# Ten score groups a batch instead of twelve, x cast at another place, the first stack DMA in three pieces, and another opening order of FFN 0

## The reference

```
x = x + 0.5 * ffn(layernorm(x))                 # "FFN 0" in the code (phase 0)
x = x + attention_block(layernorm(x))           # block = its input + gate * attention
x = x + 0.5 * ffn(layernorm(x))                 # "FFN 1" (phase 1)

ffn(y)       = (silu(y Wg^T) * (y Wu^T)) Wd^T   # 128 -> 384 -> 128, int weights / 127
attention(y) : h = rmsnorm(y) * norm_w; 4 query heads, 2 key/value heads of 32
               q, k normalised to length 1; scores = q k^T * exp(log_temperature)
               causal mask; softmax; times v; times Wo; times gate
```

## Time and profile before

| | us |
|---|---|
| median of 3 runs (lowest, highest) | 457.25 (456.99, 458.0) |
| the profiled execution | 457.19 |
| its span, first to last instruction | 455.4 |
| PE busy | 413.0 (91%) |
| ACT busy | 381.8 (84%) |
| DVE busy | 354.6 (78%) |
| POOL busy | 260.2 (57%) |
| first score of batch 0 | at 102.5 |
| first gate product of FFN 1 | at 372.95 |

### The profile page before, as it was taken

How to read it: one execution, slowest core, us unless ns; L and a number is a source line. 1 busy time by engine, 2 the same in 40 slices (tenths; PEclk the granted TensorE clock), 3 DMA queues, 4 the chain that set the end, 5 groups by cost and what they waited for, 6 DMA issues and landing times.

```text
span 455.4 us, 10469 instructions
## 1 busy us (share of the span) xinstructions
PE 413.0 (91%) x3747; PEld 213.8 (47%) x3747; DVE 354.6 (78%) x873; ACT 381.8 (84%) x545; POOL 260.2 (57%) x321
## 2 busy tenths in 40 slices
PE   0679998989998999999999999999999999999995
PEld 0346665764334335335335335335334344666654
DVE  5899997799499779689689689688556938878654
ACT  3799999667968988988988988988987999999960
POOL 5499999973544444444444444441140466998951
PEclk9999999999999999999999999999999999999999
DMA  5596433434028072074072072082070034557462
GB/s 161 127 165 150 71 48 69 71 71 97 20 51 136 1 138 51 1 129 59 0 138 46 0 138 47 1 134 54 1 140 0 2 48 57 129 95 139 93 116 74
DMA packets 119150, 34.94 MB, mean 77 GB/s; under 512 B 101568, under 2 KB 119104, under 8 KB 119104
## 3 DMA queue, kind: packets, MB, share of 16 engines
q1 hardware_dynamic: 117824, 34.02, 39.9%
q10 hardware_dynamic: 1280, 0.33, 0.3%
HBM read 4.98 MB, written 4.19 MB: 20 GB/s over the span
## 4 chain that ended last, share of the span: by engine, by line
PE 52%; issue 13%; ACT 13%; DVE 11%; POOL 7%; DMA 2%; DVEq 0%; SPq 0%; POOLq 0%; ACTq 0%
PE ps L508 11%; PE ps L709 11%; PE ps L690 9%; PE ps L714 9%; ACT XN L458 4%; PE ps L572 3%; PE ps L561 3%; ACT PT L820 3%; PE ps L597 3%; DVE H L327 2%; ACT SG L476 2%; DVE X L1024 2%; PE ps L694 2%; POOL OL L281 2%; DVE AN L1011 1%
## 5 line engine op out<-in xcount | busy, mean ns | idle before, releaser
L820 ACT ACTIVATE PT<-ps,k_exp 128x1024 f32<-128x1024 f32 (+1 forms) x192 | 162.0, 899 | 20.2 <-PE ps L694 14.8
L508 PE MATMUL ps<-XT,WT 128*128 128x512 f16 x384 | 94.4, 384 | 6.8 <-DVE H L327 2.4
L690 PE MATMUL ps<-QKT 128*128 128x512 f16 (+3 forms) x384 | 87.1, 328 | 11.4 <-ACT PT L820 9.3
L709 PE MATMUL ps<-PT,V 128*32 128x512 f32 (+3 forms) x768 | 81.8, 498 | 0.0
L714 PE MATMUL ps<-PT,ones 128*32 128x512 f32 (+3 forms) x768 | 79.6, 486 | 0.0
L433 POOL TENSOR_TENSOR HL<-H,HH 128x1024 f16<-128x1024 f32 x31 | 66.5, 2146 | 6.4 <-ACT HH L482 3.6
L327 DVE SCALAR_TENSOR_TENSOR H<-SG,k_isilu,ps 128x1536 f32<-128x1536 f32 x32 | 58.0, 1812 | 13.6 <-ACT SG L476 5.9
L281 POOL TENSOR_TENSOR OL<-ON,OH 128x512 f16<-128x512 f32 x15 | 18.2, 1215 | 77.4 <-ACT OH L277 77.4
L690 PEld LDWEIGHTS ps<-QKT 128*128 128x128 f16 x384 | 27.8, 97 | 69.3 <-ACT PT L820 60.2
L508 PEld LDWEIGHTS ps<-XT,WT 128*128 128x128 f16 x384 | 34.4, 98 | 51.8 <-issue 8.8
L458 ACT ACTIVATE XN<-X,NB,RS 128x128 f32<-128x128 f32 x128 | 52.4, 483 | 2.7 <-POOL NB L405 2.7
(11 more groups left out here) (139 smaller groups left out, 645.6 us busy)
## 6 DMA issues: line engine op xcount, KB each, us to landing
result<-X SPq DMA_DIRECT2D x15, 256.0 KB, 2.5
X<-in_L_attn_x SPq DMA_DIRECT2D x7, 512.0 KB, 4.8
X<-in_L_attn_x SPq DMA_DIRECT2D x2, 256.0 KB, 5.1
XT<-w_int SPq DMA_TRANSPOSE x32, 3.1
AXT<-AS SPq DMA_TRANSPOSE x16, 2.8
QKT<-ST SPq DMA_TRANSPOSE x16, 5.6
w_int<-in_L_ffn_w_gate SPq DMA_DIRECT2D x1, 192.0 KB, 4.2
w_int<-in_L_ffn_w_up SPq DMA_DIRECT2D x1, 192.0 KB, 4.5
```

The costliest lines, as they stand in the source:

```text
L508: i = e.matmul(out[:, j, :], WT[:, wp, w * NJ + j, :], XT[k % 2][:, xp, :], start=a == 0, stop=a == len(passes) - 1)
L690: i_ = e.matmul(o, QKT[k % 2][:, i // TPC, NH + hp, i % TPC * P:(i % TPC + 1) * P], QKT[k % 2][:, qc, 2 * hp + h, CH - n:CH], start=True, ...
L709: e.matmul(PVD[HD * h:HD * h + HD, 0, CH - n:CH], V[k % 2][:, i, v0:v0 + HD], PT[g % 2][:, h, 0:n], start=i == 0, stop=done, skip_group_ch ...
L820: e.activation(PT[g % 2][:, 2 * hp:2 * hp + 2, 0:n], SCORES[hp][:, :, 0:n], ACT.Exp, scale=k_exp[:, 0:1]).then_inc(a_exp, 1)
```

## The change

1. **Groups.** A group is now a list of tiles, each with its key tile, its offset in the score and PT buffers, and its width. In each `qc` the 384-wide and the 128-wide tile share one group (512 columns); the 256-wide tile comes last. `NG` is 10, `G0` is 3. `USES`, `MOVED` and the group numbers in ACT's program are renumbered: `("wo", 1)` in group 2, `("wo", 0)` in group 9 (the last; it was the last but one).
2. **ACT in attention.** `o_hi` of the batch before in group 1 (was 2). The squares of the second half in group 2, behind its exponentials (they were in group 1 behind the V copies). `stack_hi` in groups 4 and 5. Both `x_hi` in group 8. In batch 0 the QKV work starts in group 2 (was 3), `stack_hi` stands in groups 6 and 7, `x_hi(2)` and `x_hi(3)` in groups 0 and 1; `x_hi(2)` was ahead of the first exponentials.
3. **First stack DMA.** The DMA that turns ST[0] of batch 0 is issued as three, of two heads each: keys, first two query heads, last two. The first half of the first scores waits for the first two, the second half for the third.
4. **FFN 0's opening.** POOL makes the factors of chunks 2 to 5 one chunk at a time (was: 2 and 3 together). ACT does normalise(2) and x_hi(2) ahead of silu(0), and silu(1) ahead of h_hi(0). DVE copies the low parts r = 3, 4 behind the stats of chunk 4. Some steps of the attention's first rows and weights move by one step.

```diff
         def group(g):
             ph, c = divmod(g, NC)
-            return [0, 1, 2, 2, 3, 4][c] if g < 6 else 2 + c // 2 if not ph else NC // 2 + 2 + c // 2
+            return c if g < 6 else 3 + c // 2 if not ph else NC // 2 + 3 + c // 2
...
             def rstd_pair(k, c):
-                if not ph and c in (4, 5):
+                if not ph and 2 <= c < 6:
                     rstd(k, c, 1)
...
-            early = [(normalise, 0), (normalise, 1), (x_hi, 0), (x_hi, 1), (silu, 0)]
-            if ph:
-                early += [(normalise, 2), (x_hi, 2), (silu, 1)]
+            early = [(op, c) for c in range(3) for op in (normalise, x_hi)] + [(silu, 0), (silu, 1)]
...
-        groups = [(qc, i) for qc in range(QCS) for i in range(TPC * (qc + 1))]
+        def row_groups(qc):
+            d = TPC * qc
+            return [[(i, 0, CH)] for i in range(d + 1)] + \
+                [[(d + 1, 0, 3 * P), (d + 3, 3 * P, P)], [(d + 2, 0, 2 * P)]]
+
+        groups = [(qc, tiles_) for qc in range(QCS) for tiles_ in row_groups(qc)]
...
         USES = {0: [("qkv", 0, 0), ("qkv", 0, 1)], 1: [("qkv", 1, 0), ("qkv", 1, 1)],
-                3: [("wo", 1)], 8: [("rows", 0)], 10: [("wo", 0)], 11: [("rows", 1)]}
+                2: [("wo", 1)], 7: [("rows", 0)], 9: [("wo", 0), ("rows", 1)]}
-        MOVED = {0: [], 1: [], 3: USES[0], 4: USES[1]}
+        MOVED = {0: [], 1: [], 2: USES[0], 3: USES[1]}
...
+                if g == 0 and isinstance(b, int) and b == 0 and not shift:
+                    if hp == 0:
+                        e.wait_ge(d_k0, 16)
+                        e.wait_ge(d_q0, 16)
+                    else:
+                        e.wait_ge(d_t[0], 16)
...
-                for h in range(2):
-                    o = SCORES[hp][:, h, 0:n]
-                    i_ = e.matmul(o, QKT[k % 2][:, i // TPC, NH + hp, i % TPC * P:(i % TPC + 1) * P],
-                                  QKT[k % 2][:, qc, 2 * hp + h, CH - n:CH], start=True, stop=True)
+                for i, o, n in tiles_:
+                    for h in range(2):
+                        i_ = e.matmul(SCORES[hp][:, h, o:o + n],
+                                      QKT[k % 2][:, i // TPC, NH + hp, i % TPC * P:(i % TPC + 1) * P],
+                                      QKT[k % 2][:, qc, 2 * hp + h, CH - n:CH], start=True, stop=True,
+                                      skip_group_check=o > 0)
...
-            x_hi(2, 0)
             exps(0, 0, 0)
-            HEAD = {5: 0, 6: 1, 8: 2}
+            HEAD = {4: 0, 5: 1, 7: 2}
...
-                    if g == 2 and k >= 1:
+                    if g == 1 and k >= 1:
                         o_hi(e, b * 2 - 1)
...
-                        if k == 0 and g == 1:
-                            x_hi(3, 1)
-                        g_ = g - 3 if k == 0 else g
-                        if g_ in (0, 1):
-                            qkv_out(k + 1, m0 + g_, k, b, g_)
+                        if k == 0 and g in (0, 1):
+                            x_hi(2 + g, g)
                         g_ = g - 2 if k == 0 else g
-                        if g_ in (5, 6):
-                            stack_hi(m0 + (g_ == 6), int(g_ == 6))
-                    if k + 2 < B and g in (9, 10):
-                        x_hi(m0 + 2 + (g == 10), int(g == 10))
+                        if g_ == 0:
+                            qkv_out(k + 1, m0, k, b, 0)
+                        elif g_ == 1:
+                            for c in range(2):
+                                v_out(k + 1, m0 + 1, k, b, 1, c)
+                        elif g_ == 2:
+                            squares(k + 1, m0 + 1, k, b, 1)
+                        if g_ in (4, 5):
+                            stack_hi(m0 + (g_ == 5), int(g_ == 5))
+                    if k + 2 < B and g == NG - 2:
+                        x_hi(m0 + 2, 0)
+                        x_hi(m0 + 3, 1)
...
+                if m == 0 and not shift:
+                    stack(0, NH, NQK, d_k0)
+                    stack(0, 0, 2, d_q0)
+                    stack(0, 2, NH, d_t[0])
+                    return
...
             weights_out(1)
+            ffn_act(e, 0, [("normalise", 2), ("x_hi", 2)])
             e.wait_ge(s_wready, 1)
             ffn_act(e, 0, [("silu", 0)])
...
-            ffn_act(e, 0, None, {13: first(("v_out", 0, 0), ("v_out", 0, 1), ("squares", 0)),
+            ffn_act(e, 0, None, {0: lambda: ffn_act(e, 0, [("silu", 1)]),
+                                 13: first(("v_out", 0, 0), ("v_out", 0, 1), ("squares", 0)),
...
-            ffn_dve(e, 0, None, {-3: low_parts, -2: lambda: ffn_dve(e, 0, [("hidden", 0)]), NC - 1: stage("second")},
-                    {1: weights_scaled, 2: rows("stats", 0), 3: rows("stats", 1), 4: rows("factors", 0),
-                     5: factors_and_weights, 6: rows("factors", 2), 7: rows("factors", 3),
+            ffn_dve(e, 0, None, {-3: lambda: low_parts(2), -2: low_parts_and_hidden, NC - 1: stage("second")},
+                    {2: weights_scaled, 3: rows("stats", 0), 4: rows("stats", 1), 5: seed_and_factors,
+                     6: factors_and_weights, 7: rows("factors", 3),
```

More of the change, by code:

```diff
@@ L672, in width @@
         def width(g):
-            qc, i = groups[g]
-            return CH - max(0, i - TPC * qc) * P
+            return sum(n for _, _, n in groups[g][1])
         def att_pe(e, shift, first=None, head=None):
@@ L679, in scores @@
             def scores(k, b, g, hp):
-                qc, i = groups[g]
-                n = width(g)
+                qc, tiles_ = groups[g]
                 G = b * NG + g
@@ L696, in scores @@
                 i_.then_inc(a_s, 1)
             def weigh(k, b, g):
-                qc, i = groups[g]
-                n = width(g)
+                qc, tiles_ = groups[g]
                 G = b * NG + g
                 e.wait_ge(a_exp, 2 * G + 2)
-                again = i == 0 and k * QCS + qc >= 1
+                again = tiles_[0][0] == 0 and k * QCS + qc >= 1
                 if again:
                     e.wait_ge(a_pvc, 2 * (b * QCS + qc) - 1)
-                done = i >= TPC * qc
-                for h in range(NH):
-                    v0 = DQ + DK + HD * (h // 2)
-                    e.matmul(PVD[HD * h:HD * h + HD, 0, CH - n:CH], V[k % 2][:, i, v0:v0 + HD],
-                             PT[g % 2][:, h, 0:n], start=i == 0, stop=done, skip_group_check=True)
+                for i, o, n in tiles_:
+                    for h in range(NH):
+                        v0 = DQ + DK + HD * (h // 2)
+                        e.matmul(PVD[HD * h:HD * h + HD, 0, CH - n:CH], V[k % 2][:, i, v0:v0 + HD],
+                                 PT[g % 2][:, h, o:o + n], start=i == 0, stop=i >= TPC * qc,
+                                 skip_group_check=True)
@@ L711, in weigh @@
                 if again:
                     e.wait_ge(a_pvc, 2 * (b * QCS + qc))
-                for h in range(NH):
-                    i_ = e.matmul(PVD[HD * h:HD * h + HD, 1, CH - n:CH], ones32[:, :],
-                                  PT[g % 2][:, h, 0:n], start=i == 0, stop=done,
-                                  skip_group_check=True)
+                for i, o, n in tiles_:
+                    for h in range(NH):
+                        i_ = e.matmul(PVD[HD * h:HD * h + HD, 1, CH - n:CH], ones32[:, :],
+                                      PT[g % 2][:, h, o:o + n], start=i == 0, stop=i >= TPC * qc,
+                                      skip_group_check=True)
@@ L797, in step @@
                             use(None, None, u)
-                    if k == 0 and g == 3:
+                    if k == 0 and g == 2:
                         e.wait_ge(s_res, NC)
@@ L1236, in turn, with stack @@
         def turn(e, shift):
-            def stack(m, heads, done):
-                e.dma_start(QKT[m // QCS % 2][:, m % 2, 0:heads, :].rearrange("p h (t n) -> p (h t) n", n=P),
-                            ST[m % 2][:, 0:heads, :, :, :].rearrange("p h t s d -> p (h t) (s d)"),
+            def stack(m, lo, hi, done):
+                e.dma_start(QKT[m // QCS % 2][:, m % 2, lo:hi, :].rearrange("p h (t n) -> p (h t) n", n=P),
+                            ST[m % 2][:, lo:hi, :, :, :].rearrange("p h t s d -> p (h t) (s d)"),
                             transpose=True).then_inc(done, 16)
@@ L1447, in _, with low_parts @@
             i.then_inc(s_wprep, 1)
-            def low_parts():
-                for r in range(2, 5):
+            def low_parts(*parts):
+                for r in parts:
                     e.wait_ge(s_wpe, 3 + r)
```

27 lines of the change are left out of this document (16 added, 11 removed).

## The result

The changed kernel takes **452.11 us** (451.45 to 452.65, 4 runs) where the one before, measured beside it, takes 457.51 (456.99 to 458.0, 4 runs): a ratio of **0.988** with a 95% interval of [0.9867, 0.9894]. The prediction was 454.3 with a range of 451.0 to 457.6. The profiled execution of the changed kernel took 452.35, and its span is 450.5 for 455.40 before, so 4.9 us went (5.4 by the medians).

The account below looks back on a forecast made before the run. PE was taken to set the pace, busy 32.31 of a steady batch's 33.97 us. Opening 0, batch 0 +1.1, clock +1.7, steady batches -5.2 and batch 7 -0.5 sum to -2.9 from 457.19: 454.3 us, range 451.0 to 457.6.

Parts of the forecast that it names:

- rival A: Whole kernel: the forecast itself, 454.3 us; chance 0.42.
- FFN 0's opening, 0: FFN 0's start: POOL holds ACT's normalise(6) to its old time, so nothing changes; bounds 0.5 gained to 0.3 lost.
- Batch 0, +1.1: Batch 0: square 0.6 later, ON 0.5 more beside POOL's stack_lo, so batch 1 starts 1.1 us later; bounds 0 and 1.8.
- The clock, +1.7: Start of batch 1: after 6.3 us of PE idle the array runs at half rate, 1.7 us lost; bounds 0 and 2.9.
- Rival B: Batch 0 to 1: the clock stays up through the idle stretch, 452.6 us; chance 0.20.
- Six steady batches, -5.2: Steady batches: period 33.11 us for 33.97, 0.86 off six times; bounds 0.2 to 1.4 a batch.
- The new stalls: Steady batch on PE: waits of 0.5 before group 4's second half, 0.7 before weighing 3, 0.14 at group 5.
- the price of a merged group: PE, 384 + 128 columns: scores 1.41 us, weighing 1.86; two merges save 0.5 us a batch, bounds 0 to 0.56.
- Batch 7 and FFN 1, -0.5: Last batch: ends at 29.42 for 30.37, the weighing behind FFN 1's first gate costs 0.43 more; 0.5 us off.
- C: Steady batches: they give back only PE's own 0.5 us each, 456.5 us in all; chance 0.20.
- D: Steady batches: OH blocks ACT, later ON delays PE one for one; 34.3 us a batch, 461.3 in all; chance 0.08.
- E: FFN 0's opening: it keeps its gain on ACT since POOL catches up, 453.8 us; chance 0.10.

Follow-up runs that it names:

- the cast put first: Changed kernel with DVE's stack_hi2(2), the first stack's last cast, ahead of o_norm(0) in batch 0: 447.48 us, ratio 0.9788.
- the kept-busy version: Changed kernel with 24 unused 512-column matmuls on PE ahead of batch 1's first scores, in the DMA wait: 450.13 us, ratio 0.9853.
- The memset: Changed kernel with a 768-column fill on DVE ahead of the reciprocal of the batch before: 455.92 us, ratio 0.9964.
- the kernel with ON first: Changed kernel with DVE's o_norm ahead of the first stats and POOL's o_lo ahead of the row factors: 450.2 us, ratio 0.9857.

## Why the prediction was right, and where it was off

The sign and the range held, and rival A, the forecast, described what happened. The size was 2.0 us off in the profiled execution (-4.9 for -2.9). That is a sum of misses of both signs: the steady batches gave 2.85 more than forecast and the end 0.3 more, while batch 0 took 0.5 and the clock 0.6 more. That the time stands so near the forecast is in part luck: by the steady batches alone it would have been 451.4, near the lower bound. (The upper bound is 457.5 by its own terms, not 457.6.) Term by term:

- **FFN 0's opening, 0.** The reason held, and the size was at the edge of its bound. ACT's normalise(6) waits 0.50 for POOL's rstd(6,7) and starts at 36.01, 0.21 after its old time.

  FFN 0 as a whole is 0.34 longer from its first gate product, which itself came 0.10 later; my worst was 0.3. In the version with the old opening it is 0.19 longer than before, and with the new opening it varies by 0.35 between profiles, so not all of this is the opening's.

- **Batch 0, +1.1.** Measured +1.64 to batch 1's start, FFN 0 included. The square was foretold at 121.77 and came at 122.23. The first exponential was already 0.4 late (103.92 for 103.5), about as much as FFN 0 ended later (100.40 for 99.96), the one term that I had at nothing. ON's 1.50 is the foretold 0.5 above the 1.02 of the earlier trace rows. That the issue of the transpose sets batch 1's start is shown by the squares put back (issue 2.50 sooner, start 2.46 sooner) and by the cast put first (2.10 and 2.12). At the attention's start the first scores were not the limit (with one piece or three, the first exponential comes at the same time).
- **The clock, +1.7.** The mechanism is shown by the kept-busy version; the size was 2.29 by the stretches of the changed kernel and 2.45 by that experiment, for 1.7. I had let the half rate hold for as long as I took it to hold at the start of FFN 0, for 1.7 us of full-rate work, and the two rows there bound that only loosely. Scores, weighing and Wo all ran in it (5.31 us where 2.87 are due, so 2.44 more), within the bound of 2.9. The other four profiles with the same idle stretch lost 1.8 to 2.4 in batch 1, so part of the miss is the spread between executions. Rival B, that the clock stays up, is excluded for 6.3 us of idle.
- **Six steady batches, -5.2.** Measured -8.05 without the clock. The new stalls were the foretold ones, and the price of a merged group was right (scores 1.41 and weighing 1.86, as foretold). Three terms were mis-sized. First, in batches 2 to 5 the exponential of group 3 starts at 12.70, not 13.05: from Wo to the end of ON it took 8.98 for 9.14, and the V copies 0.96 for 1.14. The memset shows that a shift of this chain reaches the period in full (here 1.22 for 0.86, four times 0.36). Second, batch 6 has no statistics on DVE in front of the reciprocal, so ON is not late there: 32.15, about what every steady batch takes in the kernel with ON first (32.16). I priced it as a steady one and missed 0.92. Third, batch 1 was not quite steady before (34.16), and there I missed 0.53.
- **Batch 7 and FFN 1, -0.5.** The batch ends at 29.39 (forecast 29.42); behind the gate it is 0.20 later, not 0.43, so 0.78 gained.
- **C** (only PE's 0.5 a batch) fell: the periods are 32.8, not 33.4. **D** has its slope (0.78 for 0.78, in a steady batch) but not its cause: DVE's first instruction behind Wo started at once, and took its usual 0.75. **E** fell: with the old opening the time is the same (452.13 for 452.11).

What I left without a price is the square in the steady batches: the walk charged it for weighing 3's wait and did not ask what it would cost in its old place, behind an ON that now comes later. It is 0.5 us a batch.

## What to carry to other kernels

Where a batch's period follows a chain through several engines, walk that chain instruction by instruction for each kind of batch: the first, the steady and the last one had different limits here, and an instruction (the square) that gains 0.5 us a batch by stepping back in a steady batch costs 2.3 us in batch 0. A transfer that the next stage waits for is to be costed from its issue backwards, and a long idle stretch that this leaves on TensorE (6.3 us here) is to be costed twice: for its length and for the clock behind it. And one profile is one execution: before its rows explain a median, compare its time with those of the other runs.

## What the runs showed of the hardware

An idle stretch of 6.3 us in mid-kernel dropped TensorE's granted clock to half rate in all five profiles that have it (0.50 from 140 to 144), and the rate came back after some 5 us of work, for 1.8 to 2.4 us lost in the batch behind it. After shorter idle stretches it fell in some profiles and not in others. Between batches 0 and 1, 3.17 us of idle left the clock at 1.00 in one profile and 3.14 us in another did not (0.59 from 140 to 144); 2.60 and 2.56 us differ likewise. Within batch 0, after 2.11 to 2.13 us of idle before group 3, it read 0.77 and 0.81 in one profile, 0.80 and 0.77 in another, and 1.00 in two more (from 112 to 120). What decides is not shown. It shows in the times too: of six runs of the version with all squares back, one had a mean clock of 0.998 and took 450.19, the other five 0.992 to 0.994 and took 453.05 to 454.83.

A VectorE product with two SBUF inputs (ON) took 0.69 alone and 1.50 when POOL's stack_lo had started 0.22 ahead of it. The Trainium skill (SBUF — State Buffer, "SBUF: two separate sides") has an exclusive lock on the port that the two share, held by whoever starts first. By that rule stack_lo, which ended at 132.87, holds ON up, and 0.69 more is 133.56; ON ended at 133.42, so the trace agrees within 0.14. The other profiles bear it out: where ON meets a stack_lo already running, its recorded time is anything from 0.69 to 1.50, but it ends 0.54 to 0.56 after that stack_lo each time, and the 128x256 part of stack_lo that then follows takes 1.12 to 1.13 for 0.67 alone.
